# Two attention layers on one core: one of every four probability tiles of the second layer turned by DMA instead of TensorE

## Chip, cores and metric

One core of a Trainium2 chip runs one program. The metric is the device time of one execution in microseconds. The kernel before takes 691.11 us (median of 3 runs, 689.83 to 691.73).

## What is computed

Input `x` is 4 images of 256 channels by 1024 pixels, float32. Two attention layers follow each other.

```
# layer 0, per image (256 x 1024)
B, C, D = Wb @ x, Wc @ x, Wd @ x
y = gamma * D @ softmax(B.T @ C).T + x                # one 1024 x 1024 softmax

# layer 1, per image, 4 heads of 64 channels
h = group_norm(y, 32 groups) * g + b
q, k, v = wq @ h + bq, wk @ h + bk, wv @ h + bv
for head: o[head] = v[head] @ softmax(q[head].T @ k[head] / 8).T   # 1024 x 1024 each
out = y + wp @ o + bp
```

The kernel keeps nearly float32 accuracy by splitting each operand into a high part (rounded to fp32r) and a low part (the remainder), and multiplying high by high, low by high and high by low.

## The kernel before

A probability tile is 128 queries by 1024 keys. Layer 0 has 8 tiles an image, layer 1 has 32 (4 heads by 8). The product with the values needs each tile turned, keys on the partitions, as a high and a low part (`pt_hi`, `pt_lo`).

**Layer 0 turns its tiles by DMA.** GpSimd (POOL) writes `planes[...,0,:]`, the tile times 32768/rowsum in fp16 (`high_plane`, L636). VectorE (DVE) makes 32768/rowsum (`scaled_reciprocal`, L1003) and writes the fp16 remainder `planes[...,1,:]` (`plane_low`, L1010). Two DMA transposes issued by SP bring the planes to `turned` (L476, L479). ScalarE (ACT) widens the high one to `pt_hi` (L810), DVE the low one to `pt_lo` (L1166).

**Layer 1 turns its tiles on TensorE (PE).** Every engine runs through the same numbered steps, 32 an image (`image1` of each engine); the image's step `s` is written out by hand:

- PE, step s: the scores of tile s+2 (`scores1`, 4 matmuls, into one of two PSUM slots, when the exponential of tile s is done); `transpose_tile` of tile s (8 transposes into `trans`); then the groups of `STEPS1[s]`, one quarter of a value product `av` and, in 16 of the steps, a projection (`qk`, `v`, `out`).
- ACT, step s: `o_sum` of an `av` that ended in step s-1, `o_hi` of a pair (steps 5, 13, 21, 29), `trans_high` of tile s (two copies of `trans` to `pt_hi`, L747), the exponential of tile s+2 (L737), the high part of the projection of step s.
- DVE, step s: the reciprocal of tile s+1 (L982), the low part or result of the projection of step s-1, `row_max` of tile s+2 (L977), `trans_low` of tile s (two subtractions, `trans` - `pt_hi`, L995), and in steps 4, 8, 12 and so on an `o_sum` addition (L1312).
- POOL, step s: `normalise` of tile s+1 (L624, the tile by its reciprocal, in place); when there is a next image, `norm_step` (in steps 5, 9, 13, 17 a chunk of the next image's normalisation, L647, and two steps later its low part, L397); `o_lo` of a pair in steps 5, 13, 21, 29 (L401).
- SP: restacks the `q` and `k` chunks by DMA (`restack`, four DMAs each), loads the next image (`load_y`) and the residual, stores results.

Each engine runs its instructions in the order written, and waits on counting semaphores. `prob`, `scores` and `rsum` have two slots each, so tile s+2 needs what tile s used.

The projections stand in these steps: `qk7` 1, `v0` 2, `v1` 3, `v2` 5, `v3` 6, `prev_out2` 7, `prev_out3` 9 to 11, `next_qk0` 21, `out0` 22, `next_qk1` 23, `next_qk2` 25, `next_qk3` 26, `out1` 27, `next_qk4` to `next_qk6` 29 to 31.

Of the kernel before, what the change touches and what calls it, by code (L numbers as in the profile page):

```python
# [24 lines left out]
ALU = mybir.AluOpType  # L25
# [220 lines left out]
def build(nc, x, weights, vecs, out):  # L246
    y_dram = nc.dram_tensor("y_scratch", (IMAGES, KT, P, N), F32, kind="Internal").ap()
    ctx = ExitStack()
    with ctx:
# [109 lines left out]
        pt_split = sem("pt_split")  # L359
        acc_done = sem("acc_done")  # L360
# [71 lines left out]
        def _(sp):  # L432
# [48 lines left out]

            def load_inputs_of(i, half):
# [82 lines left out]
            def image1(i):  # L565
                plan = plan1(i)
                if plan.first:
                    restack(plan, "first_qk6")
                    sp.wait_ge(y_stored, FREE_CREDIT + IMAGES * 64)
                restack(plan, "qk7")  # L570
                if not plan.last:
                    sp.wait_ge(h_split, 4 * i + 4)
                    load_y(i + 1)
                if not plan.first:
                    store(plan, "prev_out2", i - 1)
                    store(plan, "prev_out3", i - 1)
                load_residual(i, 0)
                for name in plan.names:
                    if name.startswith("next_qk"):
                        restack(plan, name)  # L580
                    elif name.startswith("out"):
                        store(plan, name, i)
                load_residual(i, 1)

            image1(0)
            with sp.Fori(1, IMAGES - 1) as i:
                image1(i)
            image1(IMAGES - 1)
# [10 lines left out]
        def _(pool):  # L599
# [27 lines left out]
            def high_plane(i, t):  # L627

                if t < PLANE_SLOTS:
                    pool.wait_ge(pt_split, SPLIT_CREDIT + T0_IMAGE * i + t - PLANE_SLOTS + 1)  # L630
                else:
                    before = t - PLANE_SLOTS
                    for landed in (turned_hi, turned_lo):
                        pool.wait_ge(landed[before % TURN_SLOTS], turn_count(i, before))
                wait_scalar(rsum_ready, T0_IMAGE * i + t + 1)
                nc.gpsimd.tensor_scalar(planes[:, t % PLANE_SLOTS, 0, :], prob[:, t % 2, :],  # L636
                                        rsum[:, t % 2:t % 2 + 1], PROB_SCALE, ALU.mult, ALU.mult)\
                    .then_inc(prob_ready, 1)

# [51 lines left out]
            normalise(T1_BASE, 0)  # L691
# [11 lines left out]
            def image1(i):  # L703
                plan = plan1(i)
                for s in range(T1_IMAGE):
                    if s + 1 < T1_IMAGE - DVE_TILES or not plan.last:
                        normalise(T1_BASE + T1_IMAGE * i, s + 1)
# [16 lines left out]
        def _(act):  # L724
# [6 lines left out]
            def exp(t0, t, turned_tile=False):  # L731
                act.wait_ge(max_ready, t0 + t + 1)
                if turned_tile:
                    act.wait_ge(low_plane, t0 + t + 1)
                else:
                    act.wait_ge(transposed, TRANS_CREDIT + 2 * (t0 + t - T1_BASE) - 2)
# [4 lines left out]
            def trans_high(t0, t, av_before):  # L741

                if t % 4 == 0 and av_before is not None:
                    wait_acc(av_before)
                for h in range(2):
                    act.wait_ge(transposed, TRANS_CREDIT + 2 * (t0 + t - T1_BASE) + h + 1)
# [69 lines left out]
            def exp0(i, s):  # L816
                exp(T0_IMAGE * i, s, True)
# [60 lines left out]
            exp(T1_BASE, 0, True)  # L878
# [49 lines left out]
            exp(T1_BASE, 1, True)  # L928

            def image1(i):  # L930
                plan, t1 = plan1(i), T1_BASE + T1_IMAGE * i
                for s in range(T1_IMAGE):
                    j = s // 4
                    if j >= 2:
                        before = plan.number(f"av{j - 2}")
                    elif plan.first:
                        before = None
                    elif j == 1:
                        before = plan.number("prev_av7")
                    else:  # L940
                        before = plan.base - (LAYER1[::-1].index("av6") + 1)
# [6 lines left out]
                    trans_high(t1, s, before)  # L948
                    if s + LAG < T1_IMAGE or not plan.last:
                        exp(t1, s + LAG)  # L950
# [20 lines left out]
        def _(dve):  # L971
# [19 lines left out]
            def trans_low(t0, t):  # L991
                for h in range(2):
                    dve.wait_ge(pt_high, halves_before(t0 + t) + h + 1)
# [160 lines left out]

            def max0(i, t):
                row_max(T0_IMAGE * i, t)
# [133 lines left out]
            recip(T1_BASE, 0)  # L1290
            row_max(T1_BASE, 1)
            chunk_low(last_plan, "next_qk5", highs0(e, "next_qk5"))
# [56 lines left out]
            def image1(i):  # L1349
                plan, t1 = plan1(i), T1_BASE + T1_IMAGE * i  # L1350
                highs = HIGH_LAYER0 + (0 if plan.first else 1 + HIGH_IMAGE1 * i)
                for s in range(T1_IMAGE):
                    if s + 1 < T1_IMAGE or not plan.last:
# [13 lines left out]
                    trans_low(t1, s)  # L1367
# [33 lines left out]
        def _(pe):  # L1401
# [31 lines left out]
            def transpose_tile(t0, t, last=False):  # L1433
                if last and t >= T1_IMAGE - DVE_TILES:
                    pe.wait_ge(last_prob_ready, t - (T1_IMAGE - DVE_TILES) + 1)
                else:
                    pe.wait_ge(prob_ready, t0 + t + 1)
                for h in range(2):
                    pe.wait_ge(pt_split, halves_before(t0 + t) + h + 1)
# [212 lines left out]
            def run_groups(plan, step, i, t1):  # L1652
                for g in step:
# [13 lines left out]
                    elif name == "prev_av7":  # L1667
                        values(plan, name, part, parts, t1 - T1_IMAGE)
                    elif name.startswith("av"):
                        values(plan, name, part, parts, t1)  # L1670
# [8 lines left out]
            def side_values(side, part=0, parts=1):  # L1679

                if part == 0:

                    pe.wait_ge(pt_split, SPLIT_CREDIT + halves_before(T1_BASE + T1_IMAGE * IMAGES - 2 * (1 - side)))
# [4 lines left out]
            def image1(i):  # L1688
                plan, t1 = plan1(i), T1_BASE + T1_IMAGE * i
                for s in range(T1_IMAGE):  # L1690
# [11 lines left out]
                    transpose_tile(t1, s, plan.last)  # L1702
# [49 lines left out]
```

## Time and profile before

| | |
|---|---|
| median of 3 runs | 691.11 us |
| profiled execution | 692.13 us, span 689.5 us |
| mean granted TensorE clock | 0.992 |
| busy PE, DVE, ACT, POOL | 672.5, 561.3, 456.7, 231.2 us |
| one image of layer 1 (reciprocal of its tile 1 to that of the next image's) | 109.6 us |

The profile is of one execution; its own time is 692.13 us, 1.0 us above the median of the runs. Layer 0 ends and layer 1 begins some 250 us after the start. Busy time is the time in which an engine executes an instruction; a busy PE is not PE at its peak, as matmuls are pipelined.

### The profile page before, as it was taken

How to read it: one execution, taken by the hardware profiler on the slowest of the kernel's cores; microseconds unless marked ns; L12 is line 12 of the kernel's file. 1: busy time of each engine (PE TensorE's matmuls, PEld its weight loads, DVE VectorE, ACT ScalarE, POOL GpSimd, SP SyncE). 2: the span in 40 equal slices, each digit the busy share in tenths (PEclk: the TensorE clock that was granted, in tenths of full speed). 3: DMA queues.
4: the chain of work that ended last, by engine and by line, in shares of the span. 5: the costliest groups of instructions: out<-in, count | busy, mean ns of one | idle time of the engine just before them, and what ended most of it. 6: DMA issues, size and time to landing. Idle time of an engine off the chain costs nothing.

```text
span 689.5 us, 11125 instructions
## 1 busy us (share of the span) xinstructions
PE 672.5 (98%) x3668; PEld 571.4 (83%) x3668; DVE 561.3 (81%) x910; ACT 456.7 (66%) x790; POOL 231.2 (34%) x216
## 2 busy tenths in 40 slices
PE   8969999999999899999999999999999999999997
PEld 7858888888888688888888888888888888888886
DVE  4776667667777559999888899888899888889996
ACT  5553435434435338888777789777879778778884
POOL 0220201111115013565333556433446524324431
PEclk9989999999999999999999999999999999999999
DMA  7485657646564868001468010367200165401001
GB/s 228 92 157 110 144 94 154 150 110 137 146 144 92 187 165 212 18 1 25 111 142 213 18 46 2 77 145 182 85 31 30 46 154 123 106 16 47 1 31 61
DMA packets 96714, 69.50 MB, mean 101 GB/s; under 512 B 71072, under 2 KB 73376, under 8 KB 96672
## 3 DMA queue, kind: packets, MB, share of 16 engines
q1 hardware_dynamic: 96672, 68.97, 41.7%
q8 instruction: 22, 0.36, 0.2%
q14 instruction: 20, 0.16, 0.1%
HBM read 18.62 MB, written 8.39 MB: 39 GB/s over the span
## 4 chain that ended last, share of the span: by engine, by line
PE 85%; DVE 5%; ACT 3%; issue 3%; DMA 2%; POOL 1%; SPq 0%; POOLq 0%; DVEq 0%; ACTq 0%
PE acc L1408 37%; PE scores L1408 26%; PE trans L1442 15%; PE trans L1408 8%; DVE negmax L977 2%; ACT prob L737 1%; DVE pt_lo L995 1%; ACT pt_hi L747 1%; DMA x_raw<-in_x 1%; POOL planes L636 1%; DMA turned<-planes 1%; POOL y_in L647 0%; DVE pt_lo L1166 0%; DVE rsum L982 0%; DVE o_sum L1312 0%
## 5 line engine op out<-in xcount | busy, mean ns | idle before, releaser
L624 POOL TENSOR_SCALAR prob<-prob,rsum 128x1024 f32<-128x1024 f32 x127 | 142.8, 1124 | 258.5 <-DVE rsum L982 258.5
L737 ACT ACTIVATE prob<-scores,negmax 128x1024 f32<-128x1024 f32 x160 | 179.1, 1119 | 71.0 <-DVE negmax L977 69.4
L977 DVE TENSOR_REDUCE negmax<-scores 128x1 f32<-128x1024 f32 x160 | 194.1, 1213 | 16.8 <-PE scores L1408 15.7
L747 ACT ACTIVATE pt_hi<-trans 128x512 fp32r<-128x512 f32 x256 | 139.8, 595 | 63.5 <-PE trans L1442 62.6
L995 DVE TENSOR_TENSOR pt_lo<-trans,pt_hi 128x512 fp32r<-128x512 f32 x256 | 163.7, 681 | 1.1 <-ACT pt_hi L747 0.6
L1408 PE MATMUL scores<-k_st,q_st 128*128 128x512 f32 x512 | 137.7, 391 | 0.0
L1442 PEld LDWEIGHTS trans<-ident,prob 128*128 128x128 f32 x1024 | 117.7, 140 | 22.7 <-issue 3.8
L1442 PE MATMUL trans<-ident,prob 128*128 128x128 f32 x1024 | 134.7, 273 | 1.3 <-DVE pt_lo L995 1.1
L1408 PEld LDWEIGHTS scores<-k_st,q_st 128*128 128x128 f32 x512 | 95.8, 188 | 20.5
L1408 PE MATMUL acc<-pt_hi,v_st 128*128 128x512 f32 (+1 forms) x264 | 106.8, 407 | 0.6 <-DVE pt_lo L995 0.6
L1408 PE MATMUL acc<-pt_lo,v_st 128*128 128x512 f32 (+1 forms) x264 | 101.0, 385 | 0.0
L636 POOL TENSOR_SCALAR planes<-prob,rsum 128x1024 f16<-128x1024 f32 x32 | 36.7, 1145 | 171.5 <-DVE rsum L982 157.5
L810 ACT ACTIVATE pt_hi<-turned 128x1024 fp32r<-128x1024 f16 x32 | 33.8, 1058 | 37.1 <-DMA turned<-planes 37.1
L1408 PEld LDWEIGHTS acc<-pt_hi,v_st 128*128 128x128 f32 x264 | 49.8, 189 | 7.8 <-DVE pt_lo L995 0.8
L1408 PEld LDWEIGHTS acc<-pt_lo,v_st 128*128 128x128 f32 x264 | 49.9, 189 | 7.2
L1010 DVE SCALAR_TENSOR_TENSOR planes<-prob,rscaled,planes 128x1024 f16<-128x1024 f32 x32 | 41.5, 1297 | 14.7 <-POOL planes L636 13.9
L982 DVE RECIPROCAL rsum<-rowsum 128x1 f32<-128x1 f32 x160 | 25.8, 162 | 31.3 <-ACT prob L737 26.4
L1408 PE MATMUL scores<-x_hi,a_hi 128*128 128x512 f32 x128 | 50.0, 391 | 0.0
L1408 PE MATMUL scores<-x_hi,a_lo 128*128 128x512 f32 x128 | 49.9, 390 | 0.0
L1408 PE MATMUL scores<-x_lo,a_hi 128*128 128x512 f32 x128 | 49.8, 389 | 0.0
L737 ACT ACTIVATION_READ_ACCUMULATOR prob<-scores,negmax 128x1 f32 x160 | 31.8, 199 | 0.0
L1408 PE MATMUL acc<-pt_hi,d_hi 128*128 128x512 f32 x80 | 31.7, 396 | 0.0
(155 smaller groups left out, 1032.6 us busy)
## 6 DMA issues: line engine op xcount, KB each, us to landing
k_st<-qk SPq DMA_DIRECT2D x64, 256.0 KB, 4.7
q_st<-qk SPq DMA_DIRECT2D x64, 128.0 KB, 2.4
x_raw<-in_x SPq DMA_DIRECT2D x8, 512.0 KB, 5.4
y_out<-in_x SPq DMA_DIRECT2D x16, 256.0 KB, 3.4
y_scratch<-y_out SPq DMA_DIRECT2D x16, 256.0 KB, 2.3
y_in<-y_scratch SPq DMA_DIRECT2D x4, 1024.0 KB, 7.4
y_res<-y_scratch SPq DMA_DIRECT2D x16, 256.0 KB, 3.6
out<-y_res SPq DMA_DIRECT2D x14, 256.0 KB, 2.4
```

Source lines behind the costliest of these rows:

```text
L624: nc.gpsimd.tensor_scalar(p, p, rsum[:, t % 2:t % 2 + 1], 1.0, ALU.mult, ALU.mult)\
L636: nc.gpsimd.tensor_scalar(planes[:, t % PLANE_SLOTS, 0, :], prob[:, t % 2, :], rsum[:, t % 2:t % 2 + 1], PROB_SCALE, ALU.mult, ALU.mult)\
L737: nc.scalar.activation(prob[:, t % 2, :], scores[:, t % 2, :], ACT.Exp, bias=negmax[:, t % 2:t % 2 + 1], scale=1.0, accum_out=rowsum[:, t ...
L747: nc.scalar.activation(pt_block(pt_hi, (t // 4) % 2, t, h), trans[:, h, :].rearrange("p (j n) -> p j n", n=P), ACT.Copy).then_inc(pt_high, 1)
L810: nc.scalar.activation(pt_tile(pt_hi, t), turned[t % TURN_SLOTS][:, 0, :, :], ACT.Copy, scale=1.0 / PROB_SCALE).then_inc(pt_high, 1)
L977: nc.vector.tensor_reduce(negmax[:, t % 2:t % 2 + 1], scores[:, t % 2, :], AX_X, ALU.max, negate=True).then_inc(max_ready, 1)
L982: nc.vector.reciprocal(rsum[:, t % 2:t % 2 + 1], rowsum[:, t % 2:t % 2 + 1]).then_inc(rsum_ready, 1)
L995: nc.vector.tensor_tensor(pt_block(pt_lo, slot, t, h), trans[:, h, :].rearrange("p (j n) -> p j n", n=P), pt_block(pt_hi, slot, t, h).bitc ...
L1010: nc.vector.scalar_tensor_tensor(planes[:, t % PLANE_SLOTS, 1, :], prob[:, t % 2, :], rscaled[:, t % 2:t % 2 + 1], planes[:, t % PLANE_SLO ...
L1408: ins = nc.tensor.matmul(dst, w, m, start=(starts and n == 0), stop=(stops and n == len(pairs) - 1))
L1442: ins = nc.tensor.transpose(trans[:, h, b * P:(b + 1) * P], prob[:, t % 2, j * P:(j + 1) * P], ident[:, :])
```

## The change

In layer 1 the tiles with s % 4 == 0 (`TURNED1`), but not the last of the last image, 31 of 128, are turned as layer 0 turns its tiles:

- PE leaves out their 8 transposes, ACT and DVE their `trans_high` and `trans_low`.
- POOL writes their high plane (`high_plane1`) in the place of `normalise`, in step s-1.
- DVE makes 32768/rowsum (`scaled_reciprocal1`) and the low plane (`plane_low1`) in step s-1, the latter after `row_max` and before `trans_low` of tile s-1.
- SP issues the two DMA transposes (`turn1`) in its step s; its other DMAs are put in an order by steps, the second residual load of an image going to the start of the next one, ahead of that image's first `turn1`.
- ACT widens the high plane in step s+2 (`turned_high1`), ahead of `trans_high` of tile s+2.
- POOL widens the low plane (`turned_low1`, once ACT has done the high one) in step s+1, after the `normalise` of tile s+2 and before all else of that step.

```diff
@@ SP
+            def turn1(i, s):
+                d = turned_before(i, s)
+                slot = d % 2
+                sp.wait_ge(prob_ready, T1_BASE + T1_IMAGE * i + s + 1)
...
+                sp.dma_start_transpose(turned[slot][:, 0, :, :], planes[:, slot, 0, :]).then_inc(turned_hi[slot], 16)
+                sp.wait_ge(low_plane, PLANE_CREDIT + TILES_LAYER0 + d + 1)
+                sp.dma_start_transpose(turned[slot][:, 1, :, :], planes[:, slot, 1, :]).then_inc(turned_lo[slot], 16)
...
+                if not plan.first:
+                    load_residual(i - 1, 1)
+                for s in range(T1_IMAGE):
+                    if is_turned(i, s):
+                        turn1(i, s)
+                    if s == 3 and not plan.last:
+                        sp.wait_ge(h_split, 4 * i + 4)
+                        load_y(i + 1)
...
+                    for name in ends(STEPS1[s - 1]) if s > 0 else []:
...
+                            restack(plan, name)
...
+                if plan.has("next_qk6"):
+                    restack(plan, "next_qk6")
@@ POOL
+            def high_plane1(i, s):
...
+                wait_scalar(rsum_ready, T1_BASE + T1_IMAGE * i + s + 1)
+                nc.gpsimd.tensor_scalar(planes[:, slot, 0, :], prob[:, s % 2, :], rsum[:, s % 2:s % 2 + 1], PROB_SCALE,
+                                        ALU.mult, ALU.mult).then_inc(prob_ready, 1)
+            def turned_low1(i, s):
...
+                pool.wait_ge(pt_high, high_number(i, s))
+                wait_scalar(turned_lo[slot], turns1(i, s, 1))
+                nc.gpsimd.tensor_scalar(pt_tile(pt_lo, s), turned[slot][:, 1, :, :], 1.0 / PROB_SCALE, 1.0,
+                                        ALU.mult, ALU.mult).then_inc(turned_split, 1)
...
+                    if s + 1 < T1_IMAGE:
+                        if s + 1 < T1_IMAGE - DVE_TILES or not plan.last:
+                            normalised(i, s + 1)
...
+                    if s >= 1 and is_turned(i, s - 1):
+                        turned_low1(i, s - 1)
@@ ACT
+                elif s >= 2 and is_turned(i, s - 2):
+                    act.wait_ge(low_plane, PLANE_CREDIT + TILES_LAYER0 + turned_before(i, s - 2) + 1)
+                else:
+                    act.wait_ge(transposed, TRANS_CREDIT + 2 * transposed_before(i, s - 2) + 2)
...
+                    if s >= 2 and is_turned(i, s - 2):
+                        turned_high1(i, s - 2, av_before(s - 2))
+                    if not is_turned(i, s):
...
+                        trans_high(i, s)
@@ DVE
                     if s + 1 < T1_IMAGE or not plan.last:
                         recip(t1, s + 1)
+                        if is_turned(*behind):
+                            scaled_reciprocal1(*behind)
...
                     if s + LAG < T1_IMAGE or not plan.last:
                         row_max(t1, s + LAG)
+                    if (s + 1 < T1_IMAGE or not plan.last) and is_turned(*behind):
+                        plane_low1(*behind)
...
-                    trans_low(t1, s)
+                    if not is_turned(i, s):
+                        trans_low(i, s)
@@ PE
-                    transpose_tile(t1, s, plan.last)
+                    if not is_turned(i, s):
+                        transpose_tile(i, s, plan.last)
```

## Rows read from the trace of the kernel before

**Rows 1.** The page, busy time and share of each engine.

```profile
PE 672.5 (98%) x3668; PEld 571.4 (83%) x3668; DVE 561.3 (81%) x910; ACT 456.7 (66%) x790; POOL 231.2 (34%) x216
```

**Rows 2.** Busy time by stretch (PE, PEld, DVE, ACT, POOL, clock, DMA share, GB/s).

```profile
350.00:460.00 110.00, 109.95 (x637) 94.00 (x636) 98.00 (x159) 88.35 (x161) 48.98 (x45) 1.00 0.34 88
```

**Rows 3.** Groups of instructions: count, busy us, mean ns of one, idle before them.

```profile
L995 DVE TENSOR_TENSOR pt_lo<-trans,pt_hi 128x512 fp32r<-128x512 f32 x256 | 163.7, 681 | 1.1 <-ACT pt_hi L747 0.6
L624 POOL TENSOR_SCALAR prob<-prob,rsum 128x1024 f32<-128x1024 f32 x127 | 142.8, 1124 | 258.5 <-DVE rsum L982 258.5
L747 ACT ACTIVATE pt_hi<-trans 128x512 fp32r<-128x512 f32 x256 | 139.8, 595 | 63.5 <-PE trans L1442 62.6
L1442 PE MATMUL trans<-ident,prob 128*128 128x128 f32 x1024 | 134.7, 273 | 1.3 <-DVE pt_lo L995 1.1
L810 ACT ACTIVATE pt_hi<-turned 128x1024 fp32r<-128x1024 f16 x32 | 33.8, 1058 | 37.1 <-DMA turned<-planes 37.1
L1166 DVE TENSOR_SCALAR pt_lo<-turned 128x1024 fp32r<-128x1024 f16 x32 | 21.8, 684 | 4.7 <-DMA turned<-planes 4.7
L1321 DVE SCALAR_TENSOR_TENSOR y_res<-acc,vec,y_res 128x512 f32<-128x512 f32 x14 | 10.5, 751 | 0.1
L401 POOL TENSOR_TENSOR o_lo<-o_sum,o_hi 128x512 fp32r<-128x512 f32 x15 | 19.4, 1293 | 0.0
L647 POOL TENSOR_SCALAR y_in<-y_in,gn_now 128x512 f32<-128x512 f32 x16 | 14.1, 886 | 3.8 <-DMA y_in<-y_scratch 3.8
```

**Rows 4.** Timeline of layer 1: one tile's maximum and exponential (start, duration).

```profile
474.46 1.21 DVE L977 TENSOR_REDUCE negmax<-scores 128x1 f32<-128x1024 f32 x1
...
475.70 1.12 ACT L737 ACTIVATE prob<-scores,negmax 128x1024 f32<-128x1024 f32 x1
```

**Rows 5.** The same timeline: reciprocals on DVE, each the start of a step.

```profile
362.25 0.15 DVE L982 RECIPROCAL rsum<-rowsum 128x1 f32<-128x1 f32 x1
...
415.59 0.16 DVE L982 RECIPROCAL rsum<-rowsum 128x1 f32<-128x1 f32 x1
...
426.44 0.17 DVE L982 RECIPROCAL rsum<-rowsum 128x1 f32<-128x1 f32 x1
...
459.62 0.17 DVE L982 RECIPROCAL rsum<-rowsum 128x1 f32<-128x1 f32 x1
...
462.35 0.16 DVE L982 RECIPROCAL rsum<-rowsum 128x1 f32<-128x1 f32 x1 [0.26 <-ACT prob L737]
...
466.09 0.17 DVE L982 RECIPROCAL rsum<-rowsum 128x1 f32<-128x1 f32 x1
...
471.84 0.15 DVE L982 RECIPROCAL rsum<-rowsum 128x1 f32<-128x1 f32 x1
...
474.38 0.16 DVE L982 RECIPROCAL rsum<-rowsum 128x1 f32<-128x1 f32 x1
```

**Rows 6.** Timeline of layer 0: reciprocal, high plane and low plane of one tile.

```profile
104.20 0.16 DVE L982 RECIPROCAL rsum<-rowsum 128x1 f32<-128x1 f32 x1 [1.27 <-ACT prob L737]
...
104.56 1.12 POOL L636 TENSOR_SCALAR planes<-prob,rsum 128x1024 f16<-128x1024 f32 x1 [4.50 <-DVE rsum L982]
...
105.79 1.28 DVE L1010 SCALAR_TENSOR_TENSOR planes<-prob,rscaled,planes 128x1024 f16<-128x1024 f32 x1 [1.24 <-POOL planes L636]
```

**Rows 7.** DMA issues: median us from issue to landing.

```profile
turned<-planes SPq DMA_TRANSPOSE x64, 3.3
```

**Rows 8.** Timeline of SP at the start of image 2, layer 1.

```profile
471.30 3.42 SPq L464 DMA_DIRECT2D k_st<-qk  x4
...
474.98 2.15 SPq L558 DMA_DIRECT2D y_res<-y_scratch  x2
```

**Rows 9.** Timeline at the end of layer 0: POOL and DVE at one time.

```profile
210.61 2.48 POOL L647 TENSOR_SCALAR y_in<-y_in,gn_now 128x512 f32<-128x512 f32 x2
210.75 1.71 DVE L1010 SCALAR_TENSOR_TENSOR planes<-prob,rscaled,planes 128x1024 f16<-128x1024 f32 x1
...
216.10 2.00 POOL L636 TENSOR_SCALAR planes<-prob,rsum 128x1024 f16<-128x1024 f32 x1 [0.55 <-DVE rsum L982]
```

More of the change, by code:

```diff
@@ L566, in image1 @@
                 plan = plan1(i)
[L567 to L573, printed above, removed]
-                if not plan.first:
[L575 to L586, printed above, removed]
+                if not plan.first:
+                    load_residual(i - 1, 1)
+                for s in range(T1_IMAGE):
+                    if is_turned(i, s):
[3 more added lines that the diff above has]
+                        load_y(i + 1)
+                    if s == 15:
+                        load_residual(i, 0)
+                    for name in ends(STEPS1[s - 1]) if s > 0 else []:
+                        if not plan.has(name):
+                            continue
+                        if "qk" in name:
+                            if name == "qk7" and plan.first:
+                                sp.wait_ge(y_stored, FREE_CREDIT + IMAGES * 64)
+                            restack(plan, name)
+                        elif name.startswith("prev_out"):
+                            store(plan, name, i - 1)
+                        elif name.startswith("out"):
+                            store(plan, name, i)
+                if plan.has("next_qk6"):
+                    restack(plan, "next_qk6")
+            for i in range(IMAGES):
                 image1(i)
-            image1(IMAGES - 1)
+            load_residual(IMAGES - 1, 1)
             for side, name in enumerate(EPILOGUE_OUT):
@@ L816, in exp0, with exp1, turned_high1 @@
             def exp0(i, s):
-                exp(T0_IMAGE * i, s, True)
+                act.wait_ge(low_plane, T0_IMAGE * i + s + 1)
+                exp(T0_IMAGE * i, s)
+            def exp1(i, s):
+                if isinstance(i, int) and i == 0 and s < 2:
+                    act.wait_ge(low_plane, PLANE_CREDIT + TILES_LAYER0 + s - 1)
+                elif s >= 2 and is_turned(i, s - 2):
+                    act.wait_ge(low_plane, PLANE_CREDIT + TILES_LAYER0 + turned_before(i, s - 2) + 1)
+                else:
+                    act.wait_ge(transposed, TRANS_CREDIT + 2 * transposed_before(i, s - 2) + 2)
+                exp(T1_BASE + T1_IMAGE * i, s)
+            def turned_high1(i, s, av_before):
+                if s % 4 == 0 and av_before is not None:
+                    wait_acc(av_before)
+                slot = turned_before(0, s) % 2
+                act.wait_ge(turned_hi[slot], turns1(i, s, 1))
+                nc.scalar.activation(pt_tile(pt_hi, s), turned[slot][:, 0, :, :], ACT.Copy,
+                                     scale=1.0 / PROB_SCALE).then_inc(pt_high, 1)
             for s in range(T0_IMAGE):
@@ L926, in evacuate, with av_before @@
                         output_rows(plan, name, i)
-            exp(T1_BASE, 1, True)
+            exp1(0, 1)
             def image1(i):
                 plan, t1 = plan1(i), T1_BASE + T1_IMAGE * i
-                for s in range(T1_IMAGE):
+                def av_before(s):
                     j = s // 4
                     if j >= 2:
[L935 to L941, printed above, removed]
+                        return plan.number(f"av{j - 2}")
+                    if plan.first:
+                        return None
+                    if j == 1:
+                        return plan.number("prev_av7")
+                    return plan.base - (LAYER1[::-1].index("av6") + 1)
+                for s in range(T1_IMAGE):
                     if s >= SUM_BEHIND:
```

109 lines of the change are left out of this document (81 added, 28 removed).

## The prediction

> **What bounds the kernel now.** I read the busy shares first: PE 98%, DVE 81%, ACT 66%, POOL 34% [rows 1]. In the stretch of layer 1 PE is busy for 109.95 of 110 us, DVE for 98.0 and ACT for 88.35 [rows 2]. So PE has no gap. That alone would make each transpose taken off it a gain. The timeline then shows how near a second limit lies. DVE takes the maximum of tile s+2, ACT its exponential, and DVE begins its next step with that tile's reciprocal. From one reciprocal to the next in a step with nothing else this is 474.38 - 471.84 = 2.54 us [rows 5]: 0.08 to the maximum, 1.24 to the exponential, 1.24 until the next reciprocal [rows 4]. No buffer shortens it, as the reciprocal of a step needs the maximum of the step before. I call it the ring. PE's own plain step is also short: 4 plain steps take 426.44 - 415.59 = 10.85 us [rows 5], where the ring allows 4 x 2.54 = 10.16 and one `o_sum` addition beyond it. A step with a `qk` evacuation takes 466.09 - 462.35 = 3.74 us in the ring, one with an `o_hi` 462.35 - 459.62 = 2.73 [rows 5]. Of an image's 471.84 - 362.25 = 109.6 us [rows 5] little could be gained by a faster PE before the ring binds.
>
> **What is removed.** PE: 8 x 134.7/1024 us x 8 tiles = 1.05 us a tile, 8.4 us an image, 32.6 us for 31 tiles. DVE: 2 x 163.7/256 = 1.28 us a tile. ACT: 2 x 139.8/256 = 1.09 us [rows 3]. **What is added.** DVE: a low plane, 1.28 us [rows 6], and some 0.2 us for the scaled reciprocal; ACT: 1.06 us for the high plane; POOL: a high plane in the place of a normalisation of the same 1.12 us, and the widening of the low plane [rows 3]. So each engine's total hardly changes but PE's. What changes is where the work stands, and I go through it by steps, with R(s) for the reciprocal that opens DVE's step s, and tile s turned.
>
> *Step s-1.* DVE has recip, scaled reciprocal, maximum, low plane, `trans_low`. The low plane waits for POOL's high plane and starts 105.79 - 104.20 = 1.59 us after the reciprocal [rows 6], and with `trans_low` behind it the step ends at 1.59 + 1.22 + 1.22 = 4.03 us (back to back each takes some 0.06 less than its length), in the place of 2.54: +1.49. With a `qk` evacuation ahead it is 4.85, with one of `v` (two parts on each engine) 5.1. The exponential is hidden here, and ACT idles.
>
> *Step s.* DVE has no `trans_low`; it still has to wait for the exponential, since the ring does not shrink: 2.54 us. The 1.28 us taken off DVE is not had back; only the `o_sum` addition is now hidden, some -0.5. Here is the core of the forecast: DVE's work was moved from a step where it covered the ring into one where it doesn't.
>
> *Step s+2.* ACT has `turned_high1` (0.97 after another), `trans_high` (1.0), and the exponential (1.24): 3.2 us in the place of 2.54; +0.66 in plain steps, +0.15 where a projection was evacuated already (3.9).
>
> *POOL.* Its `turned_low1` stands in step s+1 but waits for ACT in step s+2. It ends at R(s+2) + 1.0 + 0.1 + 1.15 = 2.25. Queued behind it are the norm chunk (0.76 to 0.89, four steps an image), `o_lo` (1.29, four steps) [rows 3], and the normalisation of tile s+3, for which PE's transposes wait, and then the high plane of tile s+4, for which DVE's low plane waits. In steps with neither it is just in time. In step 13 it has both: 2.25 + 0.76 + 1.25 + 1.12 + 1.1 = 6.5 for the high plane, then low plane and `trans_low` to 9.05, where the ring alone gives 3.2 + 4.03 = 7.23: +1.8; +0.6 to +0.8 for one of them (with a projection evacuated as well the high plane is some 0.7 later, and so is the ring).
>
> The cost of `turned_low1` on POOL stands in no row. Nearest are POOL's tile operations of that size, 1.12 to 1.15; below, the same form on DVE, 0.68; above, POOL's two-input form, 1.29 for 512 elements, so 2.6 [rows 3]. I take 1.15. It is on the path in 23 of the 31 tiles: -11 us at 0.68, +33 at 2.6.
>
> *POOL beside DVE.* In steps 7, 11, 15, 19 of images 0 to 2 POOL's `h_lo` follows the high plane at once, and DVE's low plane starts 0.1 later. Where such pairs met in layer 0, a low plane took 1.71 in the place of 1.28, two norm chunks 2.48 in the place of 1.53, and a high plane 2.00 in the place of 1.12 [rows 9]. In layer 1 so far each large DVE operation reads PSUM. The bounds are 0 and the 1.29 us of `h_lo`, which reads two inputs; as it starts ahead of the low plane and overlaps nearly all of it, I take 1.15. Four such steps cost 4.0 us an image, since in step 7 a late transpose on PE hides all but 0.5. The Trainium skill (SBUF — State Buffer, SBUF: two separate sides) says that a DVE operation with two SBUF inputs and a GpSimd one that reads SBUF hold a shared port in turns, and the loser waits for the whole instruction. The rows agree that both are stretched; by the rule in full the loss would be 1.2 us a step, by the 0.43 of the row 1.6 us an image.
>
> *SP at an image's start.* The `k_st` restack ends 2.9 us after R(0), the residual load 5.3 (474.98 + 2.15 - 471.84) [rows 8]. Only then comes `turn1(0)`, landing 3.3 later [rows 7], at 8.7. ACT wants it at R(2) + 0.6 = 5.7: +3.0, at the start of images 1 to 3. The low plane lands at 10, `turned_low1` ends at 11.3; this is hidden by step 3. The other turns land in time: 6 us pass from the high plane to ACT's need.
>
> **The sum.** A plain step is 2.54, one with `qk` 3.74, one with `v` nearly the same, 3.71, one with `out` 2.54 + 0.75 [rows 3] + 0.07 = 3.36. The long pairs, in us after R(s+2):
>
> - steps 6, 7: `turned_low1` to 2.9, norm chunk 3.7, `o_lo` 5.0, normalisation 6.1, high plane 7.2, `h_lo` 8.5, low plane 9.75, `trans_low` 11.0
> - 10, 11 and 18, 19: step 10 takes 3.2; 2.05 behind it the high plane ends, `h_lo` 3.35, low plane 4.6, `trans_low` 5.75
> - 14, 15: 9.05 as above, with the port 10.3
> - 22, 23: `turned_low1` 2.9, `o_lo` 4.2, normalisation 5.3, PE's transposes 6.45, `qk1` and a quarter of `av` 8.7, scores 9.7
> - 30, 31: normalisation 5.3, high plane 6.4, low plane 7.7, `trans_low` 8.9, the low part of `qk6` 9.6, `o_sum` 10.2
>
> The steps of one image, four at a time:
> 0-3: 2.54 + 2.54 + 6.87 + 5.1 = 17.05. 4-7: 3.71 + 2.74 + 11.0 = 17.45. 8-11: 3.36 + 2.54 + 3.2 + 5.75 = 14.85. 12-15: 3.36 + 2.74 + 10.3 = 16.4. 16-19: 2.54 + 2.54 + 3.2 + 5.75 = 14.0. 20-23: 2.54 + 2.74 + 9.7 = 15.0. 24-27: 3.74 + 2.54 + 3.9 + 4.85 = 15.0. 28-31: 3.36 + 2.74 + 10.2 = 16.3.
> Together 126.1 for 109.6: +16.5. PE's own sum falls to 109.6 - 8.4 = 101.2 and never binds for long; in steps 4-7 and 20-23 I have let it add 0.7 where its scores come late behind a late transpose. Image 0 has no late start: +13.5. Images 1 and 2: +16.5 each. Image 3 has no norm chunks, no `h_lo`: +10.6. Sum +57.1. On the profiled execution's 692.1 that is 749, on the median of the runs, 691.1, it is **748 us**.
>
> **Rivals.** (a) *Faster: the 32.6 us taken from PE come through.* 691.1 - 32.6 = 658.5. It holds if DVE and ACT have slack in each step. For it: PE is at 100% and DVE at 89% of the stretch [rows 2]. Against it: the 2.54 us. It decides if steps s-1 stay under 3.1 us. (b) *DVE's total sets the pace and neighbouring steps make up for each other.* DVE's busy time grows by some 1.2 us an image; with the same 12 us of idle time as now that is +5 us, 696. Against it: two slots of scores don't let step s be shorter than the ring. (c) *No loss of POOL against DVE in layer 1*: 3 x 4.0 less, 736. (d) *`turned_low1` is slow on POOL*, 2.0 to 2.6 us: 768 to 781.
>
> **Chances.** The forecast 0.55, its own range 737 to 762; (a) 0.05, (b) 0.08, (c) 0.20, (d) 0.12. The range for 8 in 10 is 712 to 770: it reaches from (c) with the low bound of `turned_low1` (725) and some overlap of late things that I added, to half of (d). A measurement tells 0.3% from no change. Faster 0.05, same 0.03 (part of (b)), slower 0.92.
>
> **What would show it.** After: PE's transposes x776; PE at about 85% of layer 1 with idle time before its transposes, released by POOL's normalisation; DVE's steps s-1 at 4 us or more and step s at 2.54 with a wait for ACT's exponential; ACT waiting for the DMA some 3 us at the start of images 1 to 3; POOL's normalisation of tile s+3 right behind `pt_lo<-turned`; low planes of 1.7 us or more, or started late, in steps 7 to 19. Wrong: PE still at 99% in layer 1, or steps s-1 near 2.7 us.

## The result and the profile after

| | before | after |
|---|---|---|
| median | 691.12 us | 767.03 us (759.26 to 768.31, 4 runs) |
| ratio to before | | 1.1076, 95% interval 1.1012 to 1.1140 |
| profiled execution, span | 689.5 us | 757.5 us |
| mean granted TensorE clock | 0.992 | 0.973 |

The change makes the kernel 76 us slower. The profiled execution is the fastest on record; the others, at 764.9 to 768.3 us, had a mean granted clock of 0.964 to 0.966. So comparisons of medians with this kernel carry some 8 us that go with the clock, and the spans of the profiled executions are given beside them where that matters. The forecast, 748 us, was 19 us too low; its range, 712 to 770, holds the median, but the forecast's own narrower range, 737 to 762, does not.

From the page of the kernel after: busy time, the granted clock in 40 slices, and the shares by engine in the chain that ended last.

```profile
PE 671.9 (89%) x3420; PEld 555.1 (73%) x3420; DVE 576.6 (76%) x910; ACT 450.2 (59%) x759; POOL 262.7 (35%) x247
...
PEclk9989999999999999999999989999999999899999
...
PE 41%; DVE 16%; issue 13%; ACT 12%; POOL 9%; DMA 5%; SPq 3%; POOLq 0%; DVEq 0%; ACTq 0%
```

PE does 248 transposes less and its share falls from 98% to 89%, beside [rows 1]. DVE's share falls too, and ACT's. No engine is saturated: the time lies between them. In the chain that ended last PE held 85% before; now it holds 41%, and DVE, ACT, POOL, the DMA queue and plain issue share the rest.

The groups of instructions in question, columns as in [rows 3]:

```profile
L1586 PE MATMUL trans<-ident,prob 128*128 128x128 f32 x776 | 108.3, 285 | 37.3 <-POOL prob L691 35.7
...
L721 POOL TENSOR_SCALAR pt_lo<-turned 128x1024 fp32r<-128x1024 f16 x31 | 32.5, 1049 | 99.5 <-ACT pt_hi L926 96.1
L1288 DVE SCALAR_TENSOR_TENSOR planes<-prob,rscaled,planes 128x1024 f16<-128x1024 f32 x31 | 50.3, 1623 | 12.1 <-POOL planes L713 11.9
```

PE's transposes had 1.3 us of idle time ahead of them, now 37.3, released by POOL's normalisation. The widening on POOL, which no row of before showed, takes 1.05 us (1.15 was taken). The low plane in layer 1 takes 1.62 us in the mean, for 1.28 in [rows 6].

The waits that are new (who waits for whom: us in total, times, longest):

```profile
POOL pt_lo L721 <- ACT pt_hi L926: 96.1, 30, 7.4
...
PE trans L1586 <- POOL prob L691: 35.7, 20, 3.5
...
ACT pt_hi L926 <- DMA turned<-planes: 14.7, 4, 4.4
...
PE acc L1552 <- POOL o_lo L450: 8.2, 4, 2.9
```

POOL stands for 96 us at the low plane's widening, waiting for ACT's. With its queue blocked there, PE waits for the normalisation (35.7 us) and for `o_lo` (8.2 us).

The timeline of steps 14 and 15 of image 1 shows the whole chain (start, duration, engine; rows of other work left out):

```profile
438.66 1.06 ACT L926 ACTIVATE pt_hi<-turned 128x1024 fp32r<-128x1024 f16 x1
...
438.80 0.16 DVE L1102 RECIPROCAL rsum<-rowsum 128x1 f32<-128x1 f32 x1 [0.40 <-ACT prob L829]
...
439.94 1.05 POOL L721 TENSOR_SCALAR pt_lo<-turned 128x1024 fp32r<-128x1024 f16 x1 [3.61 <-ACT pt_hi L926]
...
440.97 0.77 POOL L731 TENSOR_SCALAR y_in<-y_in,gn_now 128x512 f32<-128x512 f32 x1
...
441.70 1.27 POOL L450 TENSOR_TENSOR o_lo<-o_sum,o_hi 128x512 fp32r<-128x512 f32 x1
...
441.82 0.16 DVE L1102 RECIPROCAL rsum<-rowsum 128x1 f32<-128x1 f32 x1 [0.30 <-ACT prob L829]
...
442.94 1.12 POOL L691 TENSOR_SCALAR prob<-prob,rsum 128x1024 f32<-128x1024 f32 x1
444.04 1.12 POOL L713 TENSOR_SCALAR planes<-prob,rsum 128x1024 f16<-128x1024 f32 x1
...
445.12 1.27 POOL L446 TENSOR_TENSOR h_lo<-y_in,h_hi 128x512 fp32r<-128x512 f32 x1
...
445.26 2.21 DVE L1288 SCALAR_TENSOR_TENSOR planes<-prob,rscaled,planes 128x1024 f16<-128x1024 f32 x1 [1.96 <-POOL planes L713]
...
448.60 0.15 DVE L1102 RECIPROCAL rsum<-rowsum 128x1 f32<-128x1 f32 x1
...
451.20 0.16 DVE L1102 RECIPROCAL rsum<-rowsum 128x1 f32<-128x1 f32 x1 [0.74 <-ACT prob L829]
```

The reciprocals at 438.80, 441.82 and 448.60 open DVE's steps 14, 15 and 16. `turned_high1` ends at 439.72; POOL's `turned_low1` follows at 439.94, then the norm chunk, `o_lo`, and only at 442.94 the normalisation that PE's transposes of tile 15 need, and at 444.04 the high plane of tile 16. The low plane on DVE has to wait 1.96 us for it and then runs 2.21 us beside POOL's `h_lo`. Step 15 takes 6.78 us. Step 16, with no subtraction under the ring, takes 2.60 us, DVE idle for 0.74 of them. The forecast for steps 14 and 15 was 10.3 us, measured 448.60 - 438.80 = 9.80.

The start of image 1, SP and ACT:

```profile
384.92 2.30 SPq L620 DMA_DIRECT2D y_res<-y_scratch  x2
...
387.31 1.26 SPq L540 DMA_TRANSPOSE turned<-planes  x1
...
391.90 1.06 ACT L926 ACTIVATE pt_hi<-turned 128x1024 fp32r<-128x1024 f16 x1 [4.28 <-DMA turned<-planes]
```

The residual's load keeps SP until 387.22, then comes the transpose, and ACT has its high plane at 391.90, after 4.28 us of idle time.

### The profile page after: what moved, and what is told of

Its sections match the earlier page's. It is cut to its first block, busy times and chain, and to the rows that moved or that the text cites. A ratio compares the mean times of both kernels' runs of the same rounds, so it can differ in the third digit from the quotient of the medians.

```text
span 757.5 us, 10743 instructions
## 1 busy us (share of the span) xinstructions
PE 671.9 (89%) x3420; PEld 555.1 (73%) x3420; DVE 576.6 (76%) x910; ACT 450.2 (59%) x759; POOL 262.7 (35%) x247
## 4 chain that ended last, share of the span: by engine, by line
PE 41%; DVE 16%; issue 13%; ACT 12%; POOL 9%; DMA 5%; SPq 3%; POOLq 0%; DVEq 0%; ACTq 0%
PE acc L1552 17%; PE scores L1552 13%; PE trans L1552 7%; ACT prob L829 5%; DMA turned<-planes 5%; DVE negmax L1097 4%; DVE pt_lo L1115 4%; DVE planes L1288 3%; ACT pt_hi L926 3%; POOL planes L713 3%; PE trans L1586 3%; ACT pt_hi L837 2%; POOL prob L691 2%; SPq L513 1%; POOL o_lo L450 1%
## 5 line engine op out<-in xcount | busy, mean ns | idle before, releaser
L691 POOL TENSOR_SCALAR prob<-prob,rsum 128x1024 f32<-128x1024 f32 x96 | 108.2, 1127 | 170.4 <-DVE rsum L1102 170.3
L837 ACT ACTIVATE pt_hi<-trans 128x512 fp32r<-128x512 f32 x194 | 105.9, 595 | 65.8 <-PE trans L1586 65.2
L1586 PE MATMUL trans<-ident,prob 128*128 128x128 f32 x776 | 108.3, 285 | 37.3 <-POOL prob L691 35.7
L1552 PE MATMUL scores<-k_st,q_st 128*128 128x512 f32 x512 | 140.3, 396 | 0.9 <-ACT prob L829 0.9
L1115 DVE TENSOR_TENSOR pt_lo<-trans,pt_hi 128x512 fp32r<-128x512 f32 x194 | 124.4, 681 | 16.9 <-ACT pt_hi L837 15.6
L1586 PEld LDWEIGHTS trans<-ident,prob 128*128 128x128 f32 x776 | 93.1, 146 | 58.8 <-POOL prob L691 22.6
L1552 PE MATMUL acc<-pt_hi,v_st 128*128 128x512 f32 (+1 forms) x264 | 109.2, 416 | 24.7 <-DVE pt_lo L1115 14.0
L1552 PE MATMUL acc<-pt_lo,v_st 128*128 128x512 f32 (+1 forms) x264 | 102.8, 392 | 0.0
L703 POOL TENSOR_SCALAR planes<-prob,rsum 128x1024 f16<-128x1024 f32 x32 | 36.8, 1149 | 171.6 <-DVE rsum L1102 160.9
L721 POOL TENSOR_SCALAR pt_lo<-turned 128x1024 fp32r<-128x1024 f16 x31 | 32.5, 1049 | 99.5 <-ACT pt_hi L926 96.1
L1288 DVE SCALAR_TENSOR_TENSOR planes<-prob,rscaled,planes 128x1024 f16<-128x1024 f32 x31 | 50.3, 1623 | 12.1 <-POOL planes L713 11.9
L900 ACT ACTIVATE pt_hi<-turned 128x1024 fp32r<-128x1024 f16 x32 | 33.8, 1057 | 35.7 <-DMA turned<-planes 35.4
L1130 DVE SCALAR_TENSOR_TENSOR planes<-prob,rscaled,planes 128x1024 f16<-128x1024 f32 x32 | 41.5, 1296 | 14.3 <-POOL planes L703 13.5
```

The source lines that it names most:

```text
L691: nc.gpsimd.tensor_scalar(p, p, rsum[:, t % 2:t % 2 + 1], 1.0, ALU.mult, ALU.mult)\
L721: nc.gpsimd.tensor_scalar(pt_tile(pt_lo, s), turned[slot][:, 1, :, :], 1.0 / PROB_SCALE, 1.0, ALU.mult, ALU.mult).then_inc(turned_split, 1)
L837: nc.scalar.activation(pt_block(pt_hi, (t // 4) % 2, t, h), trans[:, h, :].rearrange("p (j n) -> p j n", n=P), ACT.Copy).then_inc(pt_high, 1)
L900: nc.scalar.activation(pt_tile(pt_hi, t), turned[t % TURN_SLOTS][:, 0, :, :], ACT.Copy, scale=1.0 / PROB_SCALE).then_inc(pt_high, 1)
L1115: nc.vector.tensor_tensor(pt_block(pt_lo, slot, t, h), trans[:, h, :].rearrange("p (j n) -> p j n", n=P), pt_block(pt_hi, slot, t, h).bitc ...
L1130: nc.vector.scalar_tensor_tensor(planes[:, t % PLANE_SLOTS, 1, :], prob[:, t % 2, :], rscaled[:, t % 2:t % 2 + 1], planes[:, t % PLANE_SLO ...
```

## The experiments

Each ran in three rounds beside the kernel before, whose median was 690.9 to 691.2 us.

**PE alone, tiles 0, 4, 8 and so on.** The kernel before, where of the four transposes of a half only one is kept for these tiles:

```diff
-                    for b in range(4):
+                    for b in range(1 if t % 4 == 0 and not (last and t >= T1_IMAGE - 4) else 4):
```

> The kernel before, with 6 of the 8 transposes of every fourth tile left out on TensorE (its output is not the layer's) and everything else as it was. It gives PE 0.8 us a tile, 24 us in all, and adds nothing elsewhere. Theory (a ring of maximum, exponential and reciprocal of 2.54 us stands right behind PE): most of it is not had back, 8 to 16 us faster, 675 to 683. Rival (PE alone is the bound): the full 24 us, 667.

689.11 us, ratio 0.9979 (0.9966 to 0.9992): 1.8 us faster. Both sizes were wrong; the rival is out by far, and my own theory gave PE too much. The same stretch of layer 1 in the kernel before and in this one (busy time and count of PE, PEld, DVE, ACT, POOL; clock; DMA):

```profile
362.00:471.00 109.00, 108.95 (x630) 93.10 (x629) 97.02 (x157) 87.77 (x160) 48.97 (x44) 1.00 0.34 88
```

With the transposes left out:

```profile
362.00:471.00 109.00, 108.08 (x584) 87.76 (x583) 97.33 (x158) 88.19 (x161) 48.82 (x45) 1.00 0.34 88
```

PE ran 46 matmuls less and yet shows 108.08 of 109 us busy. Its weight loads fell from 93.10 to 87.76 us. So the 98% of the page was never a sign that PE's queue was full of work. The Trainium skill says of the matmul row (Perfetto Trace Analysis, Identifying the Most-Contended Engine) that its busy share is no good measure of how near a kernel is to its limit; it names the share of peak arithmetic and the weight load share instead. The two rows agree for the first half. In this stretch weight loads fell by 5.3 us, and the whole kernel gained 1.8 us.

**PE alone, tiles 2, 6, 10 and so on.** The same edit with `t % 4 == 2`.

> As pe_alone (6 of 8 transposes left out, the output is not the layer's), but for the tiles with s % 4 == 2 instead of 0. PE is given the same 24 us. Theory (each step is as long as the longer of PE's work and the ring; PE binds only in steps with a projection, and there is none in steps s % 4 == 0 but five in the steps 2, 6, 10 and so on): more than the 1.8 us of pe_alone, 4 to 10 us faster, 681 to 687. Rival (PE binds nowhere in layer 1): the same 1 to 2 us.

684.53 us, ratio 0.9904 (0.9887 to 0.9920): 6.4 us faster with the same amount of work left out, three and a half times as much as before. Where PE's work is taken away counts. The tiles that the change turns stand in steps with no projection, where PE is worth least. Even here three quarters of the 24 us do not arrive. The same stretch of this kernel, same columns:

```profile
362.00:471.00 109.00, 107.46 (x592) 89.41 (x591) 98.43 (x160) 88.98 (x162) 49.87 (x45) 1.00 0.35 89
```

PE still reads 107.46 of 109 us busy.

**DVE alone.** The kernel before, with DVE's work of these tiles one step earlier:

```diff
+                    if s + 1 < T1_IMAGE and moved(plan, s + 1) or s + 1 == T1_IMAGE and not plan.last:
+                        filler()   # one scalar_tensor_tensor, 128x1024, two SBUF inputs, behind row_max
...
-                    trans_low(t1, s)
+                    trans_low(t1, s, moved(plan, s))   # two columns for the moved tiles
```

> The kernel before, with DVE's two subtractions of every fourth tile cut to 2 columns (the low parts of these tiles are left out), and one operation of 128x1024 with two SBUF inputs put in one step earlier, behind the maximum. PE, ACT, POOL and SP are unchanged; DVE's total is about the same. Theory (DVE's work is moved from a step where it covered the ring to one where it is added): step s-1 some 3.8 us in plain steps, step s still 2.54; 2 to 4 us an image, 8 to 16 us slower, 699 to 707; somewhat more where it meets POOL's low part. Rival (DVE's total counts, not its place): 691.

701.55 us, ratio 1.0156 (1.0139 to 1.0172): 10.6 us slower, as the theory said. PE, DMA and POOL are given the same work. Steps 15 and 16 of image 1:

```profile
417.27 0.17 DVE L982 RECIPROCAL rsum<-rowsum 128x1 f32<-128x1 f32 x1
...
418.48 1.37 DVE L994 SCALAR_TENSOR_TENSOR turned<-planes,rscaled 128x1024 f16<-128x1024 f32 x1
418.73 2.24 POOL L397 TENSOR_TENSOR h_lo<-y_in,h_hi 128x512 fp32r<-128x512 f32 x1
...
420.96 0.15 DVE L982 RECIPROCAL rsum<-rowsum 128x1 f32<-128x1 f32 x1
...
423.52 0.17 DVE L982 RECIPROCAL rsum<-rowsum 128x1 f32<-128x1 f32 x1 [0.31 <-ACT prob L737]
```

Step 15 takes 420.96 - 417.27 = 3.69 us with the added operation in it; step 16, with DVE's subtractions gone, takes 2.56 and waits 0.31 for ACT. In the kernel before, these steps take 2.59 and 3.14 us: one grows by 1.10, the other shrinks by 0.58. The order of DVE's work costs most of the 10.6 us, but not surely all: DVE's busy time is 3.6 us higher (564.9 for 561.3), and the new operation meets POOL's `h_lo`. Two of the new operations took 2.18 us, in step 11 of images 1 and 2, which takes 4.95 us there for 3.16 before; in others, as in the row above, it was `h_lo` that took longer, 2.24 us in the place of 1.29.

**POOL's widening one step later.**

```diff
-                    if s >= 1 and is_turned(i, s - 1):
-                        turned_low1(i, s - 1)
+                    if s >= 2 and is_turned(i, s - 2):
+                        turned_low1(i, s - 2)
```

> The changed kernel, with POOL's widening of the low plane one step later, behind the normalisation of tile s+3, for which PE's transposes wait. Theory (the wait for ACT at that place holds up the norm chunk, the o_lo and the normalisation): 2 us an image from the prediction's steps 12-15, 0.6 in others, and the waits of PE's out groups for o_lo, so 12 to 20 us faster than the changed kernel, 747 to 755. Rival (POOL has slack and only moves its idle time): 767.

742.79 us (740.20 to 746.28), ratio 1.0740 (1.0713 to 1.0768): 24.2 us less than the changed kernel by the medians, 13.0 between the spans of the two profiled executions (757.5 and 744.5). The blocked POOL queue was the largest single piece by either measure; 12 to 20 us had been expected.

**`h_lo` one step later** (`s - 2` to `s - 3` in `norm_step`).

> The changed kernel, with POOL's low part of the norm chunks one step later, away from DVE's low plane. Theory (the two hold each other up for about a microsecond in steps 7, 11, 15 and 19 of images 0 to 2): DVE's low planes all take 1.28 us; 8 to 12 us faster, 755 to 759. Rival (the stretched low plane is hidden): 767.

754.90 us, ratio 1.0941 (1.0899 to 1.0983): 12.1 us less by the medians, 5.3 between the profiled spans (757.5 and 752.2). The low plane's durations (min/median/max ns), first in the kernel after:

```profile
L1288 DVE SCALAR_TENSOR_TENSOR planes<-prob,rscaled,planes x31: 1273/1284/2244, 256.1 to 723.1; 128x1024 f16<-128x1024 f32 x31
```

With `h_lo` later:

```profile
L1288 DVE SCALAR_TENSOR_TENSOR planes<-prob,rscaled,planes x31: 1274/1283/1287, 255.6 to 717.7; 128x1024 f16<-128x1024 f32 x31
```

The longest falls from 2244 to 1287 ns, and steps 11, 15 and 19 of image 1 by 0.98, 0.68 and 0.98 us. Only the low plane had been held up: the twelve `h_lo` of the kernel after took 1.27 to 1.31 us each. In step 23, where POOL has more in its queue now, 2.0 us of the gain are lost again (6.87 to 8.84).

**The next image's first turn ahead of the restack and the residual.**

```diff
                 if plan.has("next_qk6"):
+                    turn1(i + 1, 0)
                     restack(plan, "next_qk6")
```

> The changed kernel, with the DMA transposes of the next image's tile 0 issued ahead of the restack of qk6 and of the residual. Theory (the late landing holds ACT up by 3 us at the start of images 1 to 3): ACT's waits for turned planes in layer 1 fall from 14.7 us to under 3, 8 to 12 us faster, 755 to 759. Rival (the stall is hidden behind DVE's long step 3, or the restack of qk6 is now late instead): 764 to 767.

748.91 us, ratio 1.0832 (1.0814 to 1.0850): 18.1 us less by the medians, where 8 to 12 were expected, and 9.2 between the profiled spans (757.5 and 748.3). ACT's wait in layer 1 for turned planes:

```profile
ACT pt_hi L927 <- DMA turned<-planes: 1.8, 1, 1.8
```

It was 14.7 us in four waits. Steps 0 to 3 of image 1 fall from 17.94 to 13.75 us, 4.2 us; those of images 2 and 3 by 3.7 and 4.3, so 12.2 in all. Other steps became longer, where the granted clock fell in other places. The rest of the 18.1 us I can't place; a part may be the changed kernel's lower clock in its other executions.

**The three orders together.**

> The changed kernel with the three orders of pool_later, hlo_later and turn_first together. Theory (three separate mechanisms, but two of them meet in steps 6 to 19): 24 + 12 + 10 = 46 us less where they add up fully, 721; 38 to 46 less, so 721 to 729. What is then left over the kernel before, some 30 us, is the ring with the low plane (10.6 us in dve_moved) and ACT's widening in step s+2 (0.66 us or less a tile, up to 20 us). Rival (they all cure the same wait): 740.

714.51 us, ratio 1.0337 (1.0313 to 1.0360): 52.5 us less. By the medians the single effects make 24.2 + 12.1 + 18.1 = 54.4. But each of them contains the changed kernel's 767.03 us with its low clock. Between the profiled spans they are 13.0, 5.3 and 9.2, together 27.5, for 45.1 of the three orders at once (757.5 - 712.4). Shown is that each order gains by itself and that they don't cure one wait, for which 740 stood; that their effects just add up is not shown. What remains over the kernel before is 23.4 us. Reciprocals of steps 15 to 17 and the start of 18, image 1:

```profile
423.30 0.16 DVE L1103 RECIPROCAL rsum<-rowsum 128x1 f32<-128x1 f32 x1 [0.29 <-ACT prob L830]
...
427.29 0.15 DVE L1103 RECIPROCAL rsum<-rowsum 128x1 f32<-128x1 f32 x1
...
429.90 0.17 DVE L1103 RECIPROCAL rsum<-rowsum 128x1 f32<-128x1 f32 x1 [0.74 <-ACT prob L830]
...
433.78 0.16 DVE L1103 RECIPROCAL rsum<-rowsum 128x1 f32<-128x1 f32 x1 [0.40 <-ACT prob L830]
```

Step 15 takes 3.99 us (4.03 was worked out for it), step 16 takes 2.61. The 3.88 of step 17 lies in a stretch where the granted clock was 0.70 in the mean (429.90 to 433.80).

**ACT's widening in step s+3**, POOL's behind it, on top of the three orders.

> three_orders with ACT's widening of the high plane, and POOL's of the low one behind it, one step later still, in step s+3, where DVE's low plane makes the step long anyway. Theory (in step s+2 ACT's widening stands ahead of the exponential and lengthens the ring from 2.56 to 3.02): 0.45 us in plain steps, 0.1 with a projection, 4 to 8 us less than the 714.5 of three_orders, 706 to 711. Rival (POOL's widening then meets DVE's low plane, or comes late for av, and gives it back): 714 or more.

713.17 us (711.98 to 715.33), ratio 1.0331 (1.0311 to 1.0350): 1.3 us less than three_orders, inside the spread of its runs. The forecast of 4 to 8 us failed. Steps 14 and 18 of image 1 did fall, from 3.01 to 2.63 and 2.62 us, but steps 3 and 7 rose, from 4.74 to 4.97 and from 5.27 to 5.44, so little of it reaches the end.

**`trans_low` into the empty step, in steps 12, 16 and 20**, on top of the three orders.

```diff
+                    if s in (12, 16, 20):
+                        trans_low(i, s - 1)
...
+                    if s in (12, 16, 20):
+                        scores1(i, t1, s + LAG)
+                        scores1(i, t1, s + LAG + 1)
+                        transpose_tile(i, s + 1)
```

> three_orders with trans_low of tile s-1 moved into step s for s = 12, 16 and 20 alone, and there PE's scores of tile s+3 and transposes of tile s+1 ahead of the quarter of av. Theory (in these steps DVE's low plane and trans_low together make 4.0 us, and the ring of the next step covers 1.2 of them): steps 11, 15 and 19 fall from 4.0 to 2.8, step s rises from 2.6 or 3.3 to some 3.0; 0.8 us, 3 to an image, 6 to 10 us less than three_orders, 704 to 709. Rival (PE's transposes, which then wait for the moved trans_low, give it back): 714.

701.70 us, ratio 1.0158 (1.0141 to 1.0175): 12.8 us less than three_orders. Steps 15 and 16 of image 1:

```profile
419.82 0.16 DVE L1103 RECIPROCAL rsum<-rowsum 128x1 f32<-128x1 f32 x1 [0.30 <-ACT prob L830]
...
422.63 0.16 DVE L1103 RECIPROCAL rsum<-rowsum 128x1 f32<-128x1 f32 x1
...
425.63 0.14 DVE L1103 RECIPROCAL rsum<-rowsum 128x1 f32<-128x1 f32 x1
```

Step 15 is 2.81 us instead of 3.99, step 16, which now holds the subtraction, 3.00 instead of 2.61. The pair takes 5.81 us for 6.60: the 0.8 us that was worked out, 9.5 over twelve places. The rest of the 12.8 may be the clock's: it fell to 1.2 GHz six times in layer 1 of the profiled three_orders and once in this one (mean granted clock 0.978 and 0.990).

**The same in all steps, both planes widened by POOL.**

> hlo_later and turn_first, and besides: DVE's trans_low of tile s-1 moved into step s, where DVE has nothing under the ring; PE's scores of tile s+3 and transposes of tile s+1 one step earlier, ahead of the quarter of av; POOL widens both planes, the high one in step s+2 and the low one in step s+3, each behind the normalisation. ACT has nothing of it. Theory (place, not amount of work, costs the time): steps s-1 2.8 us, steps s 2.6; all of it 0 to 2 us an image over the kernel before, 688 to 700. Rival (the DMA route costs by itself, by contention or clock): above 715.

716.53 us, ratio 1.0375 (1.0358 to 1.0393), no better than three_orders. The expectation failed, and neither theory gave the reason. Steps 15 and 16 of image 1:

```profile
423.56 1.05 POOL L732 TENSOR_SCALAR pt_lo<-turned 128x1024 fp32r<-128x1024 f16 x1
...
423.69 1.98 DVE L1299 SCALAR_TENSOR_TENSOR planes<-prob,rscaled,planes 128x1024 f16<-128x1024 f32 x1
...
427.52 1.26 PE L1599 MATMUL trans<-ident,prob 128*128 128x128 f32 x8 [1.39 <-DVE pt_lo L1126]
```

POOL's widening meets DVE's low plane, which takes 1.98 us. PE's transposes wait 1.39 us for the moved subtraction. In steps with a projection this is dearer than what it saves: steps 27 and 28 of image 1 take 8.72 us for 8.22 in three_orders. The rival, a cost of the DMA route by itself, isn't shown by it either.

**The maximum ahead of the projection's evacuation, in the kernel before.**

```diff
-                    late = plan.first and s < AV_PARTS
+                    late = True
```

> The kernel before, nothing turned by DMA, with one order changed: in layer 1 DVE takes the maximum of tile s+2 ahead of the evacuation of the projection of step s-1, in all images as it was in the first four steps. Theory (the ring and not PE bounds the kernel before, as pe_alone showed; a qk evacuation lengthens it from 2.54 to 3.74 since it stands between reciprocal and maximum): those steps go to DVE's own sum, some 3.3, 3 to 6 us an image, 667 to 680, unless PE's wait for the free bank takes it. Rival (PE bounds): no change, 691, or slower by the later bank.

756.94 us, ratio 1.0951 (1.0926 to 1.0975): 66 us slower. Step 3 of image 1:

```profile
387.94 1.23 DVE L977 TENSOR_REDUCE negmax<-scores 128x1 f32<-128x1024 f32 x1 [2.37 <-PE scores L1408]
...
389.08 0.75 DVE L1300 TENSOR_TENSOR v_st<-acc,v_st 128x256 fp32r<-128x256 f32 x2
...
389.88 0.39 PE L1408 MATMUL acc<-wv_hi,h_hi 128*128 128x256 f32 x1 [1.11 <-DVE v_st L1300]
```

PE waits 1.11 us for the `acc` bank that the evacuation frees, so the scores behind it and their maximum are late; the maximum above stands behind 2.37 us of idle time of DVE for that reason. In all, DVE waits 101.4 us for scores there, 15.7 in the kernel before. So the chain that closes over a step runs through PE's `acc` banks as well. The expectation named that wait, but gave it no time.

## Why the prediction was right, and where it was off

The direction and the mechanism were right. That 767 lies in the stated range is in part luck: the range reached 770 because it took in half of rival (d), a slow widening on POOL, and that took 1.05 us, not 2.0 to 2.6. What made the time longer than 748 was something else, below.

*The ring and the place of DVE's work.* Right. Step s is 2.60 to 2.62 us in plain steps, step s-1 3.99 where nothing else disturbs it. dve_moved shows the mechanism without anything of the DMA route, at 10.6 us, of which a small part belongs to the meetings with `h_lo`.

*PE's freed time.* Right that it doesn't arrive; the prediction still took PE's busy share as a sum of work, which happened to cost nothing since the ring was laid over it. pe_alone shows it: 24 us of PE's work are worth 1.8.

*POOL.* Right in kind. pool_later gives 24.2 us in all, or 13.0 between the profiled spans. The steps where the working had these waits, 4 to 19, take 60.4 us in image 2 for 62.7 forecast. The duration was right (1.05 for 1.15). One wait was missed. PE's `out0` in step 22 needs `o_lo`, which stands behind the widening on POOL:

```profile
471.73 1.27 POOL L450 TENSOR_TENSOR o_lo<-o_sum,o_hi 128x512 fp32r<-128x512 f32 x1
...
473.12 0.49 PE L1552 MATMUL acc<-o_hi,wp_hi 128*128 128x512 f32 x1 [1.65 <-POOL o_lo L450]
```

Steps 20 to 23 take 17.69 us in image 1 for 15.0 forecast (16.39 in image 2, where the clock did not fall in them); elsewhere in image 1 the fours are within 0.9 us of the forecast: 17.94, 17.23, 14.55, 17.02, 13.87, then 17.69, 14.67, 15.96, together 128.9 for 126.1.

*POOL beside DVE.* Right in kind and near in size: the low planes take 10.6 us less with `h_lo` later (39.7 for 50.3), where 3 x 4.0 = 12.0 was forecast. That the medians differ by 12.1 is luck; the profiled spans differ by 5.3. The row of layer 0 with its 0.43 us was a poor guide to the size; the length of the other operation was the better one. By the Trainium skill's rule (SBUF — State Buffer, SBUF: two separate sides) the loser waits for all of the other's instruction. That puts the end of the low plane at 445.12 + 1.27 + 1.28 = 447.67, and it ends at 447.47; the trace agrees within 0.2 us.

*SP at an image's start.* Right in kind: 3.0 us forecast, 4.2, 3.7 and 4.3 measured. The issue began 5.45 us after R(0), nearly as worked out (5.3), but ACT could start only 4.6 us after that, not 3.3. What held the landing up, the restack's and the residual's packets ahead of it for one, no run shows.

*ACT's widening.* Its step was right (3.02 for 3.2), its worth not shown: act_later gains 1.3 us where 4 to 8 were expected.

*The sum.* In the profiled execution the four images cost 18.2, 19.3, 15.2 and 13.9 us more (13.5, 16.5, 16.5 and 10.6 forecast) and the lead into layer 1 another 1.4, 68.0 together for 57.1. Image 2, for which the steps were worked out and in which the clock fell once, came out 1.3 us below the forecast. The largest miss, 4.7 us, is image 0. The sum gave it the excess of the other images without the late start. But before the change its first twelve steps, which hold no work left by an image before, take 36.8 us against image 2's 41.5; after it they take 44.9 against 48.3, of which 3.7 are the late start. There was less in them that the longer steps could hide behind, and they cost 8.1 us, not 3.1. Image 3 came out 3.3 us above its figure, which was not worked out by steps either; in its first steps lies the longest fall of the clock.

The sum also says nothing of the clock; it took all durations at the clock of before, 1.00 in each image of layer 1. After, images 1 and 2 run the same program (busy by stretch: PE, PEld, DVE, ACT, POOL, clock, DMA share, GB/s):

```profile
381.90:510.80 128.90, 111.76 (x570) 91.58 (x569) 102.48 (x159) 86.82 (x152) 57.05 (x52) 0.95 0.49 107
510.80:635.60 124.80, 107.32 (x570) 87.25 (x569) 101.68 (x158) 86.22 (x152) 57.07 (x52) 0.99 0.49 109
```

Image 1, at 0.95, takes 4.1 us more than image 2, at 0.99; 0.5 of them come in step 2, ahead of the first fall. The granted level fell from 2.4 to 1.2 GHz in eight stretches of layer 1, four of them in image 1 and one in image 2. Before the change it did not fall in that layer while PE still had work. Ahead of each fall PE had stood idle for a good part of the time, 2.1 to 4.3 of the last 8 us. One of them, with the level of 0.50 behind it:

```profile
425.50:433.50 8.00, 5.30 (x27) 3.88 (x26) 6.96 (x10) 3.90 (x8) 5.00 (x5) 1.00 0.37 75
434.00:436.00 2.00, 2.00 (x9) 1.61 (x7) 1.00 (x3) 1.32 (x3) 0.80 (x1) 0.50 0.21 76
```

PE's busy share is nearly the same in both images, 86.7% and 86.0%, so the idle time alone does not say where the clock falls. Such a fall is seen in the steps: step 13 of image 1 takes 3.96 us for 2.62 in image 2, step 21 takes 3.76 for 2.62; in both a fall lies in image 1 and none in image 2. The same difference of clock stands between the profiled execution (0.973, 759.3 us) and the others (0.964 to 0.966, 764.9 to 768.3): some 8 of the missing 19 us go with it. No trace of the others was kept, so that share is argued and not shown.

*Left open.* plain_moved is still 10.8 us slower than the kernel before beside which it ran. Its profiled spans differ by 9.9 us: 5.7 stand in image 0, where its one fall of the clock in layer 1 lies, 1.0 and 0.8 in images 1 and 2, 1.8 in image 3, 1.1 in the lead, and the last steps are 0.4 shorter. How DVE's longer steps, the DMA traffic and the clock share in that, no run takes apart. Turning the tiles 2, 6, 10 instead, where pe_alone_2 says PE's time is worth more, was not tried. No version here that computes the two layers beats the kernel before.

## What to carry to other kernels

Before moving work off the engine with the highest share, leave some of that work out and time it: 24 us of TensorE's work were worth 1.8 us here, and the choice of tiles made that 6.4. In a pipeline of hand-ordered queues ask of each step which chain closes over it; an operation moved out of a step where it fills the chain's waiting time, into one where it comes on top, costs time though the engine's work stays the same: dve_moved's 1.28 us operation lengthened one plain step by 1.10 us and shortened the next by 0.58. And an in-order queue that waits for another engine holds up everything written behind it: put such a wait behind what others need, which was worth 24 of the 76 us lost by the medians, and 13 of 68 by the profiled spans.

## What was not expected of the hardware

- PE's busy time hardly moved, 108.95 to 108.08 of 109 us, when 46 matmuls of that stretch went; PEld's moved by 5.3 us.
- A VectorE operation of 1.28 us with two SBUF inputs took up to 2.24 us when GpSimd's 1.27 us operation had started 0.1 us ahead; GpSimd's kept its length. With the VectorE operation ahead by 0.25 us, in dve_moved, it was the other way round: 1.37 us for VectorE, 2.24 for GpSimd.
- In layer 1, where PE's longest wait for POOL was 4.0 us, the granted clock fell to 1.2 GHz in eight stretches. Executions of the one program differed by 0.009 in the mean clock and by some 8 us in time.
